# A transformer layer's projection cut into a queries-and-keys half and a values half, with the rotation ahead of the squares

## The reference

```python
def attn_layer(x, Wqkv, qs, ksc, Wo):
    qkv = x @ Wqkv
    q, k, v = jnp.split(qkv, 3, -1)
    q, k, v = (sh(q), sh(k), sh(v))          # to heads
    q = l2norm(q) * qs
    k = l2norm(k) * ksc
    q = q * cos * scale + rotate_half(q) * sin * scale
    k = k * cos * inv + rotate_half(k) * sin * inv
    out = local_attention(q, k, v)
    ...
    return out @ Wo
...
for i in range(DEPTH):
    x = attn_layer(shift_tokens(x), ...) + x
    x = ffn_layer(shift_tokens(x), ...) + x
```

## Time and profile before

| | us |
|---|---|
| median of 3 runs | 5535.63 (5527.62 to 5538.49) |
| the profiled execution | 5534.83 |
| its span, first to last instruction | 5533.5 |
| PE busy | 4968.7 (90%) |
| DVE busy | 3420.0 (62%) |
| ACT busy | 3134.8 (57%) |
| POOL busy | 2263.3 (41%) |

### The profile page before, as it was taken

How to read it: one execution, slowest core, us unless ns; L and a number is a source line. 1 busy time by engine, 2 the same in 40 slices (tenths; PEclk the granted TensorE clock), 3 DMA queues, 4 the chain that set the end, 5 groups by cost and what they waited for, 6 DMA issues and landing times.

```text
span 5533.5 us, 92962 instructions
## 1 busy us (share of the span) xinstructions
PE 4968.7 (90%) x35783; PEld 3059.1 (55%) x35848; DVE 3420.0 (62%) x6534; ACT 3134.8 (57%) x6626; POOL 2263.3 (41%) x2202
## 2 busy tenths in 40 slices
PE   5888889989898888897999999999999999999997
PEld 2223323334343433225877777777777777777775
DVE  3664566574757566675766666666666666666663
ACT  2554454434343434554767676676767766676672
POOL 1111011001010101105767676676667666666762
PEclk6999999999899989998999999999999999999998
DMA  4232222222221122311000000000000000000000
GB/s 101 45 59 43 45 51 57 37 65 45 51 49 41 35 41 48 55 31 46 21 15 21 19 24 17 23 19 22 17 23 22 19 17 22 23 19 17 22 11 31
DMA packets 125065, 189.01 MB, mean 34 GB/s; under 512 B 18800, under 2 KB 67568, under 8 KB 124400
## 3 DMA queue, kind: packets, MB, share of 16 engines
q1 hardware_dynamic: 124624, 183.06, 15.0%
HBM read 150.09 MB, written 32.51 MB: 33 GB/s over the span
## 4 chain that ended last, share of the span: by engine, by line
PE 65%; DVE 17%; ACT 9%; issue 6%; POOL 2%; DMA 1%; SPq 0%; DVEq 0%; ACTq 0%; POOLq 0%
PE psum L1208 15%; PE psum L1256 8%; PE psum L463 5%; PE psum L428 4%; PE psum L1257 4%; PE psum L449 3%; DVE maxes L649 3%; ACT probs L829 3%; PE psum L1265 2%; PE psum L1298 2%; PE psum L410 2%; PE psum L1289 2%; PE psum L1280 2%; PE psum L472 2%; DVE psum L1413 1%
## 5 line engine op out<-in xcount | busy, mean ns | idle before, releaser
L829 ACT ACTIVATE probs<-psum 128x1024 f32<-128x1024 f32 x768 | 769.7, 1020 | 639.6 <-PE psum L449 358.4
L649 DVE TENSOR_REDUCE maxes<-psum 128x1 f32<-128x1024 f32 x512 | 615.4, 1212 | 339.0 <-PE psum L428 336.1
L1399 DVE TENSOR_TENSOR lwork<-psum,rotary 128x512 f32<-128x512 f32 x384 | 265.1, 690 | 782.1 <-ACT lwork L1501 744.2
L1526 ACT ACTIVATE lprobs<-psum,small_stats,stats 128x128 f32<-128x128 f32 x1536 | 579.9, 460 | 196.6 <-DVE small_stats L1417 195.8
L1586 POOL TENSOR_TENSOR stats<-stats,minus_half 128x8 f32<-128x8 f32 x384 | 640.8, 1669 | 32.0
L1582 POOL TENSOR_TENSOR lwork<-lwork 128x512 f32<-128x512 f32 x384 | 493.6, 1285 | 327.9 <-DVE lwork L1401 327.7
L428 PE MATMUL psum<-stack 96*128 96x512 bf16 x1536 | 488.1, 401 | 139.4 <-ACT probs L829 107.6
L449 PE MATMUL psum<-stack 98*128 98x512 bf16 x1536 | 521.1, 395 | 69.6 <-DVE maxes L649 33.9
L928 POOL TENSOR_TENSOR attn<-attn,sums 128x512 f32<-128x512 f32 x48 | 60.9, 1269 | 1244.2 <-DVE sums L682 1244.2
L1501 ACT ACTIVATE lwork<-psum 128x512 f32<-128x512 f32 x384 | 231.3, 602 | 382.8 <-PE psum L1257 382.2
L646 DVE CUSTOM_DVE_ANT_0 psum<-psum,mask_by_query 128x1024 f32<-128x1024 f32 x256 | 314.1, 1228 | 204.3 <-PE psum L428 202.8
(11 more groups left out here) (228 smaller groups left out, 12506.6 us busy)
## 6 DMA issues: line engine op xcount, KB each, us to landing
stack<-k_parts SPq DMA_DIRECT2D x288, 128.0 KB
staged<-in_quads SPq DMA_DIRECT2D x144, 256.0 KB, 2.4
k_parts<-parts SPq DMA_DIRECT2D x48, 384.0 KB, 2.8
stack<-q_parts SPq DMA_DIRECT2D x288, 64.0 KB
staged<-in_w SPq DMA_DIRECT2D x54, 256.0 KB, 2.7
ctx<-in_ctxT SPq DMA_DIRECT2D x24, 512.0 KB, 4.8
q_parts<-parts SPq DMA_DIRECT2D x24, 384.0 KB, 2.8
arena<-in_ctxT SPq DMA_DIRECT2D x8, 512.0 KB, 4.1
```

The costliest lines, as they stand in the source:

```text
L649: ins = vector.tensor_reduce(to, pair(("M", u)), AX.XY, ALU.max)
L829: scalar.activation(probs[:, i % 6, :, :], pair(("E", u)), ACT.Exp).then_inc(S_["E_act"], 1)
L1526: ins = scalar.activation(pr[:, h, :], scores(u)[:, h % 2, h // 2, :], ACT.Exp, bias=st[:, 4 + h:5 + h], scale=y[:, h:h + 1])
```

## The change

The 12 matmuls of a tile are put in another order: first the six of 512 columns to the bank of queries and keys, which then signal a new semaphore `qk_pe`, then the six of 256 columns to the bank of values, which signal `qkv_pe` as before. The wait for the bank of values stands between the two sixes. DVE's three multiplications wait for `qk_pe` and no longer for the squares. ACT copies the values first and squares last, and the squares wait for DVE's multiplications (`qkv_dve`), so that the two engines don't read the bank together. The bank of queries and keys is given back by the squares (`sq_act`), and the sum of squares waits for `sq_act`.

```diff
-        LEAVES = {"qkv": ("qkv_dve", "qkv_act"), "tr": ("tr_act",), ...
+        LEAVES = {"qkv": ("sq_act", "qkv_act"), "tr": ("tr_act",), ...
@@ PE, stage qkv
-                    left(one, ("qkv", u, 0), PE)
-                    left(one, ("qkv", u, 1), PE)
-                    for c in range(C):
-                        for n, (x_, w_) in enumerate(((xs_hi, wh), (xs_hi, wl), (xs_lo, wh))):
-                            first, last = c == 0 and n == 0, c == C - 1 and n == 2
-                            tensor.matmul(qk, x_[:, c, b % 2, tok(tt)], w_[:, c * COLS:c * COLS + 512], start=first, stop=last)
-                            ins = tensor.matmul(vp[:, 0:256], x_[:, c, b % 2, tok(tt)], w_[:, c * COLS + 512:(c + 1) * COLS],
-                                                start=first, stop=last)
-                    ins.then_inc(S_["qkv_pe"], 1)
+                    for i, (to, lo, hi, sem) in enumerate(((qk, 0, 512, "qk_pe"), (vp[:, 0:256], 512, COLS, "qkv_pe"))):
+                        left(one, ("qkv", u, i), PE)
+                        for c in range(C):
+                            for n, (x_, w_) in enumerate(((xs_hi, wh), (xs_hi, wl), (xs_lo, wh))):
+                                ins = tensor.matmul(to, x_[:, c, b % 2, tok(tt)], w_[:, c * COLS + lo:c * COLS + hi],
+                                                    start=c == 0 and n == 0, stop=c == C - 1 and n == 2)
+                        ins.then_inc(S_[sem], 1)
@@ DVE, stage qkv
-                    V.wait_ge(S_["sq_act"], at_("qkv", u))
+                    V.wait_ge(S_["qk_pe"], at_("qkv", u))
@@ DVE, stage rot
-                    V.wait_ge(S_["qkv_act"], at_("qkv", u))
+                    V.wait_ge(S_["sq_act"], at_("qkv", u))
@@ ACT, stage qkv
                     A.wait_ge(S_["qkv_pe"], at_("qkv", u))
-                    left(work_at, ("sq", u), A)
-                    scalar.activation(buf("sq", u), bank(("qkv", u, 0)), ACT.Square).then_inc(S_["sq_act"], 1)
                     scalar.activation(vals[:, val_at["v", u][0], :, 0:LHD], heads(vp[:, 0:256]), ACT.Copy)
                     ...
                     scalar.activation(mixed[0:64, mix_at[u][0], :, 0:LHD], heads(vp[0:64, 0:256]), ACT.Copy).then_inc(S_["qkv_act"], 1)
+                    A.wait_ge(S_["qkv_dve"], at_("qkv", u))
+                    left(work_at, ("sq", u), A)
+                    scalar.activation(buf("sq", u), bank(("qkv", u, 0)), ACT.Square).then_inc(S_["sq_act"], 1)
```

More of the change, by code:

```diff
@@ L1089, in last_part @@
     S_ = {name: s(name) for name in (
-        "xs_act xs_pool lq_dve lq_pool rt_dve qkv_pe sq_act qkv_act qkv_dve rot_dve rot_pool tr_pe tr_act sc_pe sc_dve ex_act "
+        "xs_act xs_pool lq_dve lq_pool rt_dve qk_pe qkv_pe sq_act qkv_act qkv_dve rot_dve rot_pool tr_pe tr_act sc_pe sc_dve ex_act "
         "pt_pe pt_act pv_pe pv_dve ot_pe ot_act ot_dve add_pe add_dve fa_pe fa_dve fa_act fa_pool fb_pe fb_dve fb_pool fy_pe fy_dve fc_act fc_dve "
@@ L1124, in last_part @@
         ONE = {"qkv": 2, "tr": 1, "pt": 1, "pv": 1, "ot": 1, "wo": 2, "fa": 1, "fb": 1, "fy": 1, "fh": 2, "fw": 1}
-        LEAVES = {"qkv": ("qkv_dve", "qkv_act"), "tr": ("tr_act",), "pt": ("pt_act",), "pv": ("pv_dve",), "ot": ("ot_dve",), "wo": ("add_dve", "add_dve"),
+        LEAVES = {"qkv": ("sq_act", "qkv_act"), "tr": ("tr_act",), "pt": ("pt_act",), "pv": ("pv_dve",), "ot": ("ot_dve",), "wo": ("add_dve", "add_dve"),
                   "fa": ("fa_dve",), "fb": ("fb_dve",), "fy": ("fy_dve",)}
```

## The result

The changed kernel takes 5494.7 us (5493.3 to 5504.4, 4 runs) where the one before takes 5537.1 (5527.6 to 5541.6, 4 runs): a ratio of 0.9929, 95% interval 0.9912 to 0.9947. It is faster by 0.7%, some 42 us; 64 were forecast, and 5494.7 lies at the upper edge of the forecast's own range (5445 to 5495). The profiled execution took 5493.38 us, with a span of 5491.8 against 5533.5. Timed once more beside other kernels it had the ratio 0.9942 (0.9929 to 0.9955), 31 us.

What follows compares the result with a forecast made beforehand. PE was taken to bound the kernel, its stalls being waits for banks. Terms A -60, B -24, C +6 and D +14 sum to -64 us, from 5534.8 to 5471; own range 5445 to 5495, whole range 5440 to 5515.

Steps and rivals of the forecast that it cites:

- rival 1: Turns behind the up projections go at ACT's pace, so at most 51 us less 17.6 is won: 5501; chance 0.16.
- waits for `lprobs` of tens of microseconds: Sign that the forecast is wrong: PE waits for `lprobs`, `turned` or `queries` appear with tens of microseconds.
- The work on PE: PE's 12 matmuls per tile stay at 2.1 us, six short ones in a row 0.12 us apart: cost 0.
- rival 3: Six short matmuls in a row go at the pace of the weight load: +161 us, giving 5632; chance 0.02.
- Term A: The projection's 66 stalls for the bank of `att_lo` go, as that wait moves behind six matmuls: -60 us.
- Term B: Stage pv behind the up projections gets its bank earlier, shortening 33 stalls and ending 22: -24 us, bounds 0 and -33.
- Term D: Projections behind a layer norm start 0.60 to 0.65 us later, squares waiting for DVE: +14 us, bounds 8 and 50.
- Term C: Turns behind the up projections: with PE ahead, late ACT costs 0.25 us, 22 to 26 times: +6 us.
- where PE does not wait, DVE's earlier rotation only moves its idle time: Elsewhere, in turns without PE stalls, rotating earlier on DVE neither wins nor loses time: cost 0.
- The sum of squares: DVE's sum of squares waits for `sq_act`, 1.7 us after the projection's end, but comes after the maximum: cost 0.
- Rival 2: In 84 tiles ACT stands before its squares because DVE may be late, reaching PE: 5606, slower; chance 0.08.
- The rule of the Trainium skill: Repeated gaps mean lacking SBUF or PSUM room; no bank is added, so only about 5525 us would be reached.

Runs made afterwards that it cites:

- PE's order alone: Only PE's matmul order and the place of the values' bank wait changed, against the kernel before: 5479.9 us, 0.9908; timed again 5484.8, 0.9919.
- the last experiment: The whole change plus one moved wait: POOL's first subtraction also waits for DVE's second cast; 5467.2 us, 0.9881 against the kernel before.
- squares first: PE's part as in the change, but ACT squares once queries and keys are there, DVE rotates after; 5445.5 us, 0.9845 against the kernel before, again 5440.2, 0.9844.

## Why the prediction was right, and where it was not

The sign, the place and three of the four terms held; one term was sized far too small. That the time still fell into the forecast's own range, by 0.3 us, is partly luck: it is nearer to rival 1's 5501 than to 5471. One of the prediction's own signs of being wrong came too, waits for `lprobs` of tens of microseconds: 21.4 us.

- **The work on PE**: right. The short matmuls stand at 0.12 us apart, and rival 3 is out.
- **Term A** (-60): right in its mechanism, and by itself. PE's order alone brought -56 and -44 (the last part: -50 and -48), with 8 us of idle time handed on to the output projection and 6 to the waits for `lprobs`. The sentence that the split covers the stalls without any help of DVE is what that experiment shows.
- **Term B** (-24): right. 33 stalls were forecast to stay, each with 0.27 us, and 33 do, with 0.26; 33.0 - 8.7 = 24.3 us of idle time.
- **Term D** (+14): about right. Behind a norm PE stands longer. The row that answers to the last of the earlier trace rows, in the kernel after, reads

```profile
3601.20 0.80 PE L1255 MATMUL psum<-wqkv_hi,xs_hi 128*128 128x512 f32 x1 [2.21 <-ACT lwork L1506]
```

  That is 2.21 us idle for 1.58, 0.63 more; 0.60 to 0.65 was forecast. Over all 26 such waits, 40.2 us in the last experiment, where no others are left, against 22.8 + 3.6: +13.8.
- **Term C** (+6): this is the step that failed. It said that ahead of ACT's pace PE loses 0.25 us in 22 to 26 turns. Two things were there. The waits for `lprobs` rose from 6.6 us in 12 turns to 21.4 us in 50, +15. And 22 projections behind the products wait for the squares, 55.7 - 40.2 = 15.5 us idle, with the 0.25 us of each, 5.5, some 21 us. The second is not ACT's pace but the cast on DVE that POOL holds up, which no term had. In sum +36 and not +6, and -60 - 24 + 36 + 14 gives -34, between the measured -42 and -31.

With the cast out of the way (the last experiment) the waits for `lprobs` are 17.3 us, +11 for ACT's pace. The sum is then -60 - 24 + 11 + 14 = -59, and the measured time is 61 us below the kernel before (the last part 71 us). So for a kernel without the collision the forecast of -64 would have been close.

The sentence "where PE does not wait, DVE's earlier rotation only moves its idle time" was wrong for this reason: it also moved POOL against DVE, by 0.05 us at the place that mattered, and this made a cast 1.1 us longer. I had priced what a later DVE costs and not what an earlier POOL meets. The sum of squares, put at no cost in the same paragraph, waits for ACT 25 times, 5.8 us in all; part of the 0.60 us above is spent there.

The Trainium skill (SBUF — State Buffer, section "Who interferes with whom") has DVE and GpSimd share one pair of ports under an exclusive lock, where the one that starts first keeps it for its whole instruction; on DVE this concerns, among others, operations in a mode with two ports, which a cast can enter. No run shows whether this cast is in that mode. The rows agree in both directions: 1.56 us for 0.43 where POOL was first, with the cast ending 0.30 us after POOL's operation, and 1.52 for 1.27 where DVE was. They don't agree for every operation of POOL: in the kernel before, 90 casts of DVE in the last part overlap the raising to a power (L1586) and no other operation of POOL of 0.2 us or more, and none of them takes more than 0.43 us.

Rival 2, in which ACT stands behind DVE and the kernel gets slower, did not happen to the change, but is a real mechanism: with the squares ahead of the copies it made 1.0058. Rival 1 is the part of term C that goes by `lprobs`; it is real, with 11 to 15 us, but it does not cap the gain, since squares first wins some 90 us. The rule of the Trainium skill (Perfetto Trace Analysis, section "Optimization Strategy") alone would have left 5525; all three groups of stalls were waits for banks, as it says, but asking for one later was enough.

## What to carry to other kernels

Where an engine waits for several buffers ahead of a group of instructions, wait for each just before the first instruction that needs it; here this alone brought 44 to 56 us, for 14 us of idle time that came back in other places. When two engines read the same data one after the other, start the first on the part that is ready first, and don't make the engine that has more queued behind it stand in line for the other (the squares behind DVE, 1.0058). And when an engine is made earlier, look at which operations of its neighbour now start at the same time as its own; a mean duration that rises between two profiles (442 to 615 ns) is the sign, and one moved wait gave back 31 us here.

## What the runs showed of the hardware

A cast of 512 fp32 columns from SBUF to SBUF on DVE takes 0.43 us, and up to 1.56 us when POOL's subtraction (L1599) began 0.01 us before it; when the cast began 0.04 us first, it was POOL's that grew from 1.27 to 1.52 us. A shift of 0.05 us between two engines thus decides over 1.1 us, 22 times in this kernel. DVE's multiplications that read PSUM show no such thing: L1399 before and L1397 after, the same operation, take 690 and 686 ns on average. Casts of weights may: the 36 of `wout_hi` take 20.3 us before and 31.2 after, and still 31.2 with POOL's wait moved, with no wait of PE that names them. How far other operations of DVE are open to it was not tried.
